# Sums of the attention weights behind the second half of P V, their rest on VectorE, in a four-layer cross-attention kernel

## The chip, the cores and the metric

The kernel runs on one core of a Trainium2 chip. The metric is the device time of one execution in microseconds (us). A core has five engines with instruction streams of their own: TensorE (PE; its weight loads are listed as PEld), VectorE (DVE), ScalarE (ACT), GpSimd (POOL) and SyncE (SP, which here issues the DMAs). They meet only at semaphores. PE writes to PSUM, in banks; DVE and ACT read those.

## What is computed

Four cross-attention layers run one after the other on x (4 batches, 512 tokens, 256 channels), each against the same context (4 batches, 1024 tokens, 512 channels). Layers 0, 2 and 3 are alike ("wide": 16 heads of 64), layer 1 has an RMS norm and grouped keys. Cut to what matters:

```python
def wide_layer(x, ctx, mask_A, mask_B, Wq, Wk, Wv, Wo, bo, tok_A, tok_B):
    q, k, v = x @ Wq, ctx @ Wk, ctx @ Wv                 # 16 heads of 64
    logits = einsum('bhqd,bhkd->bhqk', q, k) / 8
    logits += col_bias                                   # -20 * (1 - mask) in the columns tok_A, tok_B
    probs = softmax(logits, axis=-1)
    out = einsum('bhqk,bhkd->bhqd', probs, v)
    return out @ Wo + bo + x

x = wide_layer(x, ...)
x = x + attention(rmsnorm(x, norm_w) @ wq, ctx @ wk, ctx @ wv) @ wo   # 16 query heads, 4 key heads, of 16
x = wide_layer(x, ...)
x = wide_layer(x, ...)
```

The softmax is made as exp(logit - max), then P V, then a division by the sum of the exponentials over the 1024 keys. The change is about these sums.

## The kernel before

**Items and slots.** The work is cut into 112 items. A wide item p is a pair of heads for one batch (8 pairs x 4 batches in each wide layer); items 32 to 47 are the grouped layer. The program runs through slots s = -2 to 111. Slot s computes the scores, exponentials and first half of P V of item s, and finishes item s - 1 (second half of P V, sums, normalisation, output projection). It also projects queries and keys of item s + 2 and values of item s + 1, and takes the score maxima of item s + 1. Nothing is scheduled by a planner: each engine's stream is written out by hand, slot by slot.

**Turned slots.** All wide slots except 29 to 31 and 111 are of the form that the function turned_slot writes (111 is a shorter one of its own). On PE its order is: score block 0; the second half of P V of item s - 1 (attend, L1094, fp32, 16 matmuls); score block 1; the sums of item s - 1 (sums, L1140); then the projections of queries (project_q), keys (project_k) and values; score block 2; out projection and first half of P V; score block 3. A score block is four extra matmuls (L1039: minus the maximum and the token bias), two for the maxima of the next item ("opening", L986), twelve for the scores (L1054), and two more for maxima ("closing", L986).

**The sums.** POOL adds the eight blocks of exponentials into acc (add, L742). ACT then writes acc in f16 (sums_hi: acc_h, printed as tile sq, L1589). POOL subtracts this from acc and writes the rest in f16 (sums_lo: acc_l, also printed as sq, L754, semaphore s_acc_l). PE multiplies both by ones (L1140, 128*64 tiles) into a bank of ps_j. ACT copies that bank to rinv (sums_out, L1598, semaphore s_sum_sb), DVE takes the reciprocals (L2082), POOL multiplies o_un by them (L771). On ACT, sums_hi stands behind the exponentials of block 0, and sums_out behind the exponentials of block 1.

**P V.** The first half goes from PSUM to o_un by ACT; the second half is added to it by DVE (second_half, L2073, semaphore s_o_un), which frees its bank.

**Banks.** ps_j has two banks that nearly everything on PE takes in turn. bank_users lists the users in the order of PE's program with the bank of each (f, 1 - f, a, 1 - a: 0 or 1 by the slot's parity), and take puts a wait in front of each user for the reader of the bank's last user: s_o_un behind a second half of P V, s_sum_sb behind sums, s_max behind maxima, and so on. The opening maxima of a block use one bank of ps_j (kind "mx").

**Special slots.** For the first four items of a wide layer x is split in halves of precision in the same slots (splits_x); in slots 8 to 12 and 52 to 56 DVE also makes the token rows of a later layer, one step each (token_rows).

Of the kernel before, what the change touches and what calls it, by code (L numbers as in the profile page):

```python
# [15 lines left out]
ALU = mybir.AluOpType  # L16
# [41 lines left out]
def grouped(p):  # L58
    return G0 <= p < G1
# [107 lines left out]
def turned(s):  # L167

    return 0 <= s < N - 1 and not grouped(s) and not G0 - 3 <= s < G0


def splits_x(s):

    p = s + 2
    return p < N and not grouped(p) and p - STARTS[layer_of(p)] < B
# [22 lines left out]
def split_sums(p):  # L198

    return not grouped(p) and not G0 - 3 <= p < G0  # L200
# [9 lines left out]
    return sum(thirds(q) for q in range(p))  # L210


def splits(p):

    return wides(p) - min(max(p - (G0 - 3), 0), 3)
# [7 lines left out]
def bank_users():  # L223

    users = []
    turns = 0

    def then(kind, p, bank=None):
        users.append((kind, p, (1 - users[-1][2] if users else 0) if bank is None else bank))

    for s in range(-2, N):
        now, nxt, far, past = 0 <= s < N, 0 <= s + 1 < N, 0 <= s + 2 < N, 0 <= s - 1 < N
        if s == N - 1:
            then("pvb", s - 1, 0)
            then("sum", s - 1, 1)
            then("out0", s - 1, 0)
            then("out1", s - 1, 1)
            continue
        if turned(s):
            f = turns % 2  # L240
            turns += 1

            def opening(i, bank):
                for p, u in passes(s)[2 * i]:
                    then("mx", units(p) + u, bank)

            a = int(not splits_x(s)) ^ f
            opening(0, f)
            if far and splits_x(s):
                then("k0", s + 2, 1 - f)  # L250
            if past:
                then("sum" if grouped(s - 1) else "pvb", s - 1, a)
            opening(1, 1 - a)
            if past:
                then("rb" if grouped(s - 1) else "sum", s - 1, a)
            if far:
                then("q0", s + 2, 1 - a)
                if not splits_x(s):
                    then("k0", s + 2, 1 - f)
                then("k1", s + 2, f)  # L260
            if nxt:
                then("v0", s + 1, 1 - f)
            opening(2, f)
            if past:
                then("out0", s - 1, f)
            then("pva", s, 1 - f)
            opening(3, f)
            if nxt:
                then("v1", s + 1, 1 - f)
                then("nm0", s + 1, f)  # L270
            if past:
                then("out1", s - 1, f)
            continue
        if s == -1:
            for kind, p, bank in (("bias", 2, 0), ("v0", 0, 1), ("bias", 3, 0), ("bias", 4, 0), ("k0", 1, 1), ("bias", 5, 0),
                                  ("bias", 6, 0), ("k1", 1, 1), ("bias", 7, 0), ("q0", 1, 0), ("v1", 0, 1), ("nm0", 0, 0)):
                then(kind, p, bank)
            continue
        if not grouped(s):
            if rms_batch(s) is not None:  # L280
                then("ms", rms_batch(s), 0)
                then("pvb", s - 1, 1)
                then("k0", s + 2, 1)
            else:
                if past:
                    then("sum" if grouped(s - 1) else "pvb", s - 1)
                if far:
                    then("k0", s + 2)
            if s < 0:
                then("q0", s + 2)  # L290
                then("k1", s + 2)
            if past:
                then("rb" if grouped(s - 1) else "sum", s - 1)
            if s >= 0:
                if nxt and has_values(s + 1):
                    then("v0", s + 1)
                if far:
                    then("k1", s + 2)
                    if not late_queries(s):
                        then("q0", s + 2)  # L300
            if past:
                then("out0", s - 1)
            if now:
                then("pva", s)
            if past:
                then("out1", s - 1)
            if nxt and has_values(s + 1):
                then("v1", s + 1)
            if nxt and not grouped(s + 1):
                then("nm0", s + 1)  # L310
            if late_queries(s):
                then("q0", s + 2)
                then("q1", s + 2)
            if s == -2:
                then("bias", 0)
                then("bias", 1)
            continue
        if s == G0:
            then("pvb", s - 1, 0)
            then("k0", s + 2, 1)  # L320
            then("ms", rms_batch(s), 0)
            then("sum", s - 1, 0)
            then("v0", s + 1, 1)
            then("nm0", s, 0)
            then("nm1", s, 0)
            then("v1", s + 1, 0)
            then("k1", s + 2, 1)
            then("pv", s, 0)
            then("out0", s - 1, 1)
            then("out1", s - 1, 1)  # L330
            then("q0", s + 2, 1)
            then("q1", s + 2, 1)
            then("ms", rms_batch(s + 1), 1)
            continue
        if s > G0 + 1:
            then("out1", s - 2, 1)
        then("nm0", s, 1)
        then("nm1", s, 1)
        if has_values(s + 2):
            then("k0", s + 2, 1)  # L340
            then("sum", s - 1, 0)
            then("k1", s + 2, 1)
        else:
            then("sum", s - 1, 1)
        then("pv", s, 0)
        then("rb", s - 1, 1)
        if has_values(s + 1) and grouped(s + 1):
            then("v0", s + 1, 1)
        if early_bias(s) is not None:
            then("bias", early_bias(s), 1)  # L350
        then("q0", s + 2, 1)
        if has_values(s + 1) and grouped(s + 1):
            then("v1", s + 1, 1)
        if grouped(s + 2):
            then("q1", s + 2, 1)
        then("out0", s - 1, 1)
        if s == G1 - 1:
            then("out1", s - 1, 1)
            then("v0", s + 1, 1)
            then("v1", s + 1, 1)  # L360
            then("nm0", s + 1, 1)
    return users
# [8 lines left out]
def build(nc, a, out):  # L371
    with ExitStack() as ctx:
# [30 lines left out]
        acc = sb("acc", [P, 2, 2 * TQ], F32)  # L403
# [38 lines left out]
        acc_h, acc_l = halves[:, 0:2 * TQ], halves[:, 2 * TQ:4 * TQ]  # L442
# [246 lines left out]
        def _(pool):  # L689
# [108 lines left out]
            for s in range(-2, N - 1):  # L798
# [12 lines left out]
                splitting = s >= 0 and far and layer_of(s + 2) != GROUPED and s + 2 - STARTS[layer_of(s + 2)] < B  # L811
                if splitting:
                    split_x_hi(layer_of(s + 2), batch_of(s + 2))
                if past and split_sums(s - 1):
                    sums_lo(s - 1)
                if splitting:
                    split_x_lo(layer_of(s + 2), batch_of(s + 2))
# [33 lines left out]
        def _(pe):  # L851
# [299 lines left out]
            def rows_of_reciprocals(p):  # L1151

                pe.wait_ge(s_r_x, groups(p) + 1)
                dst = take("rb", p)
                for t in range(QT):
                    last = MM(dst[:, t * P:(t + 1) * P], rinv[:, t * P:(t + 1) * P], unit[:], start=True, stop=True)  # L1156
                last.then_inc(s_rb, 1)
# [114 lines left out]
            def turned_slot(s):  # L1272
# [20 lines left out]
                    project_k(s + 2, 0)  # L1293
                if past and not grouped(s - 1):
                    attend(s - 1, 1)
                elif past:
                    sums(s - 1)
                score_block(1)
                if past and not grouped(s - 1):
                    sums(s - 1)  # L1300
                elif past:
                    rows_of_reciprocals(s - 1)
                if far:
                    project_q(s + 2, 0)
                    if not splits_x(s):
# [616 lines left out]
        def _(dve):  # L1922
# [77 lines left out]
            def keys_lo(p, half):  # L2000
                r, keys = p % 3, slice(half * HALF, (half + 1) * HALF)
                dve.wait_ge(s_k_h, values_before(p) + 1 + half)
                if G1 <= p < G1 + 3:
                    dve.wait_ge(s_kb, 16 * builds_before(G1))
                to = all_keys(batch_of(p), half) if grouped(p) else k_l[:, r, keys]
                split_lo(to, bank(f"k{half}", p), 1 / WS, k_h[:, r, keys]).then_inc(s_k_l, 1)
# [56 lines left out]
            def extra_rows(p):  # L2063
# [2 lines left out]
                V.scalar_tensor_tensor(ext_q[:, p % 2, :], bank("nm0", p), flag(FLAG_M), bias_q[:], ALU.mult, ALU.add  # L2066
                                       ).then_inc(s_ext_q, 1)

            def second_half(p):
                dve.wait_ge(s_pvb, wides(p) + 1)  # L2070
                dve.wait_ge(s_pva_sb, wides(p) + 1)
                o = o_un[:, p % 2, :]
                V.tensor_tensor(o, bank("pvb", p), o, ALU.add).then_inc(s_o_un, 1)  # L2073
# [121 lines left out]
            def turned_slot(s):  # L2195
# [13 lines left out]
                        token_rows(w, s - start)  # L2209
                if far and splits_x(s):  # L2210
                    keys_lo(s + 2, 0)
                if past and not grouped(s - 1):
                    second_half(s - 1)
                elif past:
                    reciprocal_by_query(s - 1)
# [204 lines left out]
```

## Time and profile before

| What | us |
|---|---|
| median of 3 runs | 3433.31 |
| lowest, highest | 3433.3, 3434.82 |
| the profiled execution | 3431.57 |
| its span, first to last instruction | 3429.4 |
| PE busy in it | 3297.0 |
| DVE, POOL, ACT busy | 2537.5, 2497.7, 2194.5 |

The profile is of one execution. The page adds up busy times by engine and follows the chain of work that ended last; windows give the busy time of each engine in a stretch; timelines list instructions in order of time, neighbours of one form merged into one row, with the idle time before them in brackets and who ended it. PEclk is the granted clock of TensorE as a share of 2.4 GHz. A busy matmul's end is modelled; the distance from one start to the next is the safer measure.

### The profile page before, as it was taken

Reading aid. Unit: us, or ns where it says so; the run is one execution under the profiler, and the core shown is the slowest. Engines: PE = TensorE matmul, PEld = TensorE weight load, DVE = VectorE, ACT = ScalarE, POOL = GpSimd, SP = SyncE. Lnnn points to the kernel's source line nnn. Section 1 sums busy time; section 2 is a strip of 40 time slices with the busy share of each in tenths; the row PEclk is TensorE's granted clock in tenths of the full one; section 3 lists DMA queues with packets and bytes.
Section 4 is the critical chain, followed back from the end, with each engine's and each line's share of the span. In section 5 each row is a group of like instructions: output and inputs, shape, how many; then the busy total and the mean of one; then the engine's idle time right before and its main releaser. Section 6 shows DMA issues by size and latency. Waiting matters only on the chain.

```text
span 3429.4 us, 72971 instructions
## 1 busy us (share of the span) xinstructions
PE 3297.0 (96%) x28066; PEld 1558.9 (45%) x28066; DVE 2537.5 (74%) x4678; ACT 2194.5 (64%) x2698; POOL 2497.7 (73%) x1206
## 2 busy tenths in 40 slices
PE   6999999999987888889999999999999999999998
PEld 3444545445432322234454544445444544445553
DVE  6677877777766788856787777777667777777776
ACT  5466666666545677764666666666546666666665
POOL 6888888888741000028888888888888888888887
PEclk9999999999998999999999999999999999999999
DMA  4000000000000000000000000000000000000000
GB/s 157 1 11 11 1 11 11 11 2 9 6 10 12 8 13 17 17 1 11 11 1 11 11 11 2 11 11 11 1 11 11 1 11 11 11 2 11 3 2 26
DMA packets 50195, 42.29 MB, mean 12 GB/s; under 512 B 4928, under 2 KB 42176, under 8 KB 49856
## 3 DMA queue, kind: packets, MB, share of 16 engines
q1 hardware_dynamic: 49136, 37.08, 3.6%
q8 instruction: 231, 3.78, 0.5%
q14 instruction: 108, 0.88, 0.1%
q10 hardware_dynamic: 720, 0.53, 0.1%
HBM read 32.36 MB, written 2.10 MB: 10 GB/s over the span
## 4 chain that ended last, share of the span: by engine, by line
PE 90%; ACT 3%; DVE 3%; issue 2%; POOL 2%; DMA 0%; SPq 0%; ACTq 0%; DVEq 0%; POOLq 0%
PE ps_j L903 39%; PE ps_st L1054 13%; PE ps_j L1094 11%; PE ps_j L1107 6%; PE ps_sm L986 6%; PE ps_st L1039 3%; PE ps_j L1081 3%; ACT pt L1582 2%; PE ps_sm L1068 2%; PE ps_j L1140 1%; PE ps_st L986 1%; POOL acc L742 1%; PE ps_j L995 1%; PE ps_j L1156 1%; PE ps_j L1131 0%
## 5 line engine op out<-in xcount | busy, mean ns | idle before, releaser
L742 POOL TENSOR_TENSOR acc<-acc,pt 128x1024 f32<-128x1024 f32 x570 | 1365.0, 2395 | 261.9 <-ACT pt L1582 207.2
L1582 ACT ACTIVATE pt<-ps_st 128x1024 f32<-128x1024 f32 x768 | 742.9, 1019 | 300.8 <-PE ps_st L1054 288.9
L2045 DVE CUSTOM_DVE_ANT_0 ps_sm<-ps_sm,bias_m,nmx 128x512 f32<-128x512 f32 x666 | 479.9, 756 | 185.3 <-PE ps_j L986 149.3
L903 PE MATMUL ps_j<-w_h,ctx_h 128*128 128x128 f16 x3072 | 530.5, 219 | 2.3 <-ACT rinv L1598 1.1
L903 PE MATMUL ps_j<-w_l,ctx_h 128*128 128x128 f16 x3072 | 529.4, 219 | 0.0
L903 PE MATMUL ps_j<-w_h,ctx_l 128*128 128x128 f16 x3072 | 529.4, 219 | 0.0
L2045 DVE CUSTOM_DVE_ANT_0 ps_sm<-ps_sm,bias_m 128x512 f32<-128x512 f32 x486 | 334.7, 707 | 158.6 <-PE ps_j L986 147.3
L1094 PE MATMUL ps_j<-pt,v 128*64 128x512 f32 x1792 | 409.2, 598 | 1.3 <-DVE q_l L1933 1.3
L771 POOL TENSOR_TENSOR o_un<-o_un,rinv 128x512 f32<-128x512 f32 x111 | 142.0, 1280 | 336.9 <-ACT rinv L1594 291.1
L2082 DVE RECIPROCAL rinv<-rinv 128x256 f32<-128x256 f32 x190 | 331.3, 1746 | 14.1 <-ACT rinv L1598 4.4
L2035 DVE TENSOR_REDUCE nmg<-ps_st 128x2 f32<-128x1024 f32 x248 | 296.0, 1218 | 45.2 <-PE ps_st L986 43.8
L1582 ACT ACTIVATE pt<-ps_sm 128x1024 f32<-128x1024 f32 x256 | 261.4, 1021 | 101.5 <-PE ps_sm L1068 101.4
L903 PEld LDWEIGHTS ps_j<-w_h,ctx_h 128*128 128x128 f16 x3072 | 300.4, 98 | 55.6 <-issue 40.1
L903 PE MATMUL ps_j<-ctx_h,w_h 128*128 128x512 f16 x800 | 304.4, 380 | 16.9 <-DVE w_l L1933 12.7
L1559 ACT ACTIVATE p_h<-pt 128x1024 f16<-128x1024 f32 x312 | 319.7, 1052 | 0.0
L903 PEld LDWEIGHTS ps_j<-w_l,ctx_h 128*128 128x128 f16 x3072 | 300.7, 98 | 10.7
L903 PE MATMUL ps_j<-ctx_l,w_h 128*128 128x512 f16 x800 | 304.0, 380 | 0.0
L903 PE MATMUL ps_j<-ctx_h,w_l 128*128 128x512 f16 x800 | 303.8, 380 | 0.0
L986 PE MATMUL ps_sm<-k_h,q_h 64*128 64x512 f16 x1160 | 293.8, 380 | 9.2 <-DVE nmx L2045 6.9
L903 PEld LDWEIGHTS ps_j<-w_h,ctx_l 128*128 128x128 f16 x3072 | 300.6, 98 | 0.0
L754 POOL TENSOR_TENSOR sq<-acc,sq 128x1024 f16<-128x1024 f32 x92 | 198.6, 2159 | 118.4 <-ACT sq L1589 118.4
L1054 PE MATMUL ps_st<-q_h,k_l 64*128 64x512 f16 x1488 | 283.0, 377 | 0.0
(201 smaller groups left out, 6603.0 us busy)
## 6 DMA issues: line engine op xcount, KB each, us to landing
w_raw<-wk SPq DMA_DIRECT2D x25, 256.0 KB, 2.9
pt<-ctx_t SPq DMA_DIRECT2D x6, 1024.0 KB, 7.2
w_raw<-wv SPq DMA_DIRECT2D x24, 256.0 KB, 3.6
wo_raw<-wo SPq DMA_DIRECT2D x28, 128.0 KB, 2.0
w_raw<-wq SPq DMA_DIRECT2D x24, 128.0 KB, 3.0
k_h<-k_l SPq DMA_DIRECT2D x72, 32.0 KB, 2.0
x<-x_t SPq DMA_DIRECT2D x4, 512.0 KB, 8.3
acc<-ctx_t SPq DMA_DIRECT2D x2, 1024.0 KB, 9.1
```

The lines of the kernel that those rows point to most:

```text
L742: G.tensor_tensor(total, first, pt[:, n % RING, :], ALU.add).then_inc(s_acc, 1)
L754: G.tensor_tensor(acc_l, acc[:, p % 2, :], acc_h, ALU.subtract).then_inc(s_acc_l, 1)
L903: done = MM(dst, l, r, start=first and i == 0, stop=last and i == n - 1)
L986: last = MM(dst[h], queries_in(p, tile)[d, t * P:(t + 1) * P], k_h[d, r, half * HALF:(half + 1) * HALF], start=True, stop=True)
L1054: last = MM(ps_st[:, side, h, :], k[d, r, keys], q[d, r, :], start=False, stop=n == 2)
L1094: last = MM(dst[h * HD:(h + 1) * HD, :], values_of(p)[:, kt, h * HD:(h + 1) * HD], pt[:, (units(p) + kt) % RING, h * TQ:(h + 1) * TQ], sta ...
L1107: last = MM(dst[h * HD:(h + 1) * HD, :], v[:, p % 2, kt, h * HD:(h + 1) * HD], weights[:, h * TQ:(h + 1) * TQ], start=start, stop=stop)
L1559: A(p_h[:, kt, :], pt[:, n % RING, :], ACT.Copy).then_inc(s_p_h, 1)
L1582: A(pt[:, n % RING, :], src.rearrange("p h q -> p (h q)"), ACT.Exp).then_inc(s_exp, 1)
L2035: V.tensor_reduce(nmg[:, half, t, 2 * tile:2 * tile + 2], maxima_in(p, u), AX_X, ALU.max, negate=True).then_inc(s_max, 1)
L2045: last = V.tensor_tensor_reduce(out=src, in0=src, in1=bias_m[:, t, half * HALF:(half + 1) * HALF], scale=-1.0, scalar=nmx[:, 0, t, h:h + 1 ...
L2082: V.reciprocal(r, r).then_inc(s_rinv, 1)
```

## The change

In 84 slots (2 to 28, 50 to 77, 82 to 110; early_sums(s - 1) names them) three things are different:

- PE's sums of item s - 1 stand directly behind the second half of P V, ahead of score block 1. In bank_users the sums take bank 1 - a, and the opening maxima of block 1 take bank a, the other way round than before; q0 stays on 1 - a.
- acc_l is written by DVE, ahead of second_half, instead of by POOL.
- POOL waits for s_acc_l where its subtraction stood.

ACT's program is as it was.

```diff
--- before.py
+++ after.py
@@ -210,6 +210,11 @@
     return sum(thirds(q) for q in range(p))
 
 
+def early_sums(p):
+
+    return not grouped(p) and turned(p + 1) and not splits_x(p + 1)
+
+
 def splits(p):
 
     return wides(p) - min(max(p - (G0 - 3), 0), 3)
@@ -248,11 +253,16 @@
             opening(0, f)
             if far and splits_x(s):
                 then("k0", s + 2, 1 - f)
-            if past:
-                then("sum" if grouped(s - 1) else "pvb", s - 1, a)
-            opening(1, 1 - a)
-            if past:
-                then("rb" if grouped(s - 1) else "sum", s - 1, a)
+            if past and early_sums(s - 1):
+                then("pvb", s - 1, a)
+                then("sum", s - 1, 1 - a)
+                opening(1, a)
+            else:
+                if past:
+                    then("sum" if grouped(s - 1) else "pvb", s - 1, a)
+                opening(1, 1 - a)
+                if past:
+                    then("rb" if grouped(s - 1) else "sum", s - 1, a)
             if far:
                 then("q0", s + 2, 1 - a)
                 if not splits_x(s):
@@ -811,7 +821,9 @@
                 splitting = s >= 0 and far and layer_of(s + 2) != GROUPED and s + 2 - STARTS[layer_of(s + 2)] < B
                 if splitting:
                     split_x_hi(layer_of(s + 2), batch_of(s + 2))
-                if past and split_sums(s - 1):
+                if past and early_sums(s - 1):
+                    pool.wait_ge(s_acc_l, splits(s - 1) + 1)
+                elif past and split_sums(s - 1):
                     sums_lo(s - 1)
                 if splitting:
                     split_x_lo(layer_of(s + 2), batch_of(s + 2))
@@ -1293,13 +1305,13 @@
                     project_k(s + 2, 0)
                 if past and not grouped(s - 1):
                     attend(s - 1, 1)
-                elif past:
+                if past and (grouped(s - 1) or early_sums(s - 1)):
                     sums(s - 1)
                 score_block(1)
-                if past and not grouped(s - 1):
+                if past and grouped(s - 1):
+                    rows_of_reciprocals(s - 1)
+                elif past and not early_sums(s - 1):
                     sums(s - 1)
-                elif past:
-                    rows_of_reciprocals(s - 1)
                 if far:
                     project_q(s + 2, 0)
                     if not splits_x(s):
@@ -2066,6 +2078,10 @@
                 V.scalar_tensor_tensor(ext_q[:, p % 2, :], bank("nm0", p), flag(FLAG_M), bias_q[:], ALU.mult, ALU.add
                                        ).then_inc(s_ext_q, 1)
 
+            def sums_lo(p):
+                dve.wait_ge(s_acc_h, splits(p) + 1)
+                V.tensor_tensor(acc_l, acc[:, p % 2, :], acc_h, ALU.subtract).then_inc(s_acc_l, 1)
+
             def second_half(p):
                 dve.wait_ge(s_pvb, wides(p) + 1)
                 dve.wait_ge(s_pva_sb, wides(p) + 1)
@@ -2209,6 +2225,8 @@
                         token_rows(w, s - start)
                 if far and splits_x(s):
                     keys_lo(s + 2, 0)
+                if past and early_sums(s - 1):
+                    sums_lo(s - 1)
                 if past and not grouped(s - 1):
                     second_half(s - 1)
                 elif past:
```

PE in slot 26, from the second half of P V to the query projection (rows of the same form left out; s_sum_sb: rinv copied by ACT; s_o_un: second half added by DVE; s_acc_l: rest of acc written). Before:

```order
L1094 MATMUL ps_j<-pt,v 64x512 [waits s_x,s_v_sb,s_exp]
L1039 MATMUL ps_st<-ext_q,ext_k 128x512 [waits s_exp]
L986 MATMUL ps_sm<-k_h,q_h 128x512 [waits s_max,s_q_h,s_k_h]
L986 MATMUL ps_j<-k_h,q_h 128x512
L1054 MATMUL ps_st<-q_h,k_h 128x512 x2
L986 MATMUL ps_sm<-k_h,q_h 128x512 [waits s_max,s_q_h,s_k_h]
L986 MATMUL ps_sm<-k_h,q_h 128x512 [waits s_max_a]
L1140 MATMUL ps_j<-sq,ones_h_sb 64x512 [waits s_o_un,s_acc_l]
L1140 MATMUL ps_j<-sq,ones_h_sb 64x512 x3
L903 MATMUL ps_j<-xh,w_h 128x512 [waits s_max,s_xs,s_w_l]
L903 MATMUL ps_j<-xl,w_h 128x512
```

After, in the changed file's line numbers:

```order
L1106 MATMUL ps_j<-pt,v 64x512 [waits s_x,s_v_sb,s_exp]
L1152 MATMUL ps_j<-sq,ones_h_sb 64x512 [waits s_max,s_acc_l]
L1152 MATMUL ps_j<-sq,ones_h_sb 64x512 x3
L1051 MATMUL ps_st<-ext_q,ext_k 128x512 [waits s_exp]
L998 MATMUL ps_sm<-k_h,q_h 128x512 [waits s_max,s_o_un,s_q_h,s_k_h]
L998 MATMUL ps_j<-k_h,q_h 128x512
L1066 MATMUL ps_st<-q_h,k_h 128x512 x2
L998 MATMUL ps_sm<-k_h,q_h 128x512 [waits s_max,s_q_h,s_k_h]
L998 MATMUL ps_sm<-k_h,q_h 128x512 [waits s_max_a]
L915 MATMUL ps_j<-xh,w_h 128x512 [waits s_sum_sb,s_xs,s_w_l]
L915 MATMUL ps_j<-xl,w_h 128x512
```

The sums (ones_h_sb) moved up by one score block. The wait for s_o_un moved from the sums to the opening maxima, and the query projection (inputs xh,w_h) now waits for s_sum_sb, where it waited for s_max.

DVE in slot 26, from the closing maxima of block 0 to the first maxima of block 1. Before:

```order
L2045 ISA ps_sm,nmx<-ps_sm,bias_m,nmx 128x512 [waits s_max,s_bias_sb,s_nm16,s_max_mm]
L2045 ISA nmx 128x1
L2045 ISA ps_sm,nmx<-ps_sm,bias_m,nmx 128x512
L2045 ISA nmx 128x1
L2073 TENSOR_TENSOR o_un<-ps_j,o_un 128x512 [waits s_pva_sb,s_pvb]
L2045 ISA ps_sm,nmx<-ps_sm,bias_m 128x512 [waits s_bias_sb,s_max_mm]
```

After:

```order
L2057 ISA ps_sm,nmx<-ps_sm,bias_m,nmx 128x512 [waits s_max,s_bias_sb,s_nm16,s_max_mm]
L2057 ISA nmx 128x1
L2057 ISA ps_sm,nmx<-ps_sm,bias_m,nmx 128x512
L2057 ISA nmx 128x1
L2083 TENSOR_TENSOR sq<-acc,sq 128x1024 [waits s_acc_h]
L2089 TENSOR_TENSOR o_un<-ps_j,o_un 128x512 [waits s_pva_sb,s_pvb]
L2057 ISA ps_sm,nmx<-ps_sm,bias_m 128x512 [waits s_bias_sb,s_max_mm]
```

One subtraction (sq is acc_l, written from acc and acc_h) came in between the maxima and second_half (o_un).

POOL in slot 26, from the last adds of item 25 to the normalisation (o_un). Before:

```order
L742 TENSOR_TENSOR acc<-acc,pt 128x1024 [waits s_acc,s_exp] x4
L754 TENSOR_TENSOR sq<-acc,sq 128x1024 [waits s_acc_h]
L742 TENSOR_TENSOR acc<-pt 128x1024 [waits s_sum,s_exp]
L742 TENSOR_TENSOR acc<-acc,pt 128x1024 [waits s_acc,s_exp] x2
L771 TENSOR_TENSOR o_un<-o_un,rinv 128x512 [waits s_o_un,s_rinv]
```

After:

```order
L752 TENSOR_TENSOR acc<-acc,pt 128x1024 [waits s_acc,s_exp] x4
L752 TENSOR_TENSOR acc<-pt 128x1024 [waits s_sum,s_exp,s_acc_l]
L752 TENSOR_TENSOR acc<-acc,pt 128x1024 [waits s_acc,s_exp] x2
L781 TENSOR_TENSOR o_un<-o_un,rinv 128x512 [waits s_o_un,s_rinv]
L759 TENSOR_TENSOR p_l<-pt,p_h 128x1024 [waits s_p_h]
```

The subtraction is gone, and the first add of item 26 waits for s_acc_l too.

## Rows read from the trace of the kernel before

**Rows 1.** Page: busy us by engine, and the chain that ended last

```profile
PE 3297.0 (96%) x28066; PEld 1558.9 (45%) x28066; DVE 2537.5 (74%) x4678; ACT 2194.5 (64%) x2698; POOL 2497.7 (73%) x1206
...
PE 90%; ACT 3%; DVE 3%; issue 2%; POOL 2%; DMA 0%; SPq 0%; ACTq 0%; DVEq 0%; POOLq 0%
```

**Rows 2.** Windows: length, busy (count) of PE, PEld, DVE, ACT, POOL; then PEclk

```profile
794.85:824.15 29.30, 29.21 (x262) 14.61 (x261) 21.99 (x45) 19.41 (x25) 25.05 (x13) 1.00 0.01 2
```

**Rows 3.** Timeline of PE, slot 26: start, us, engine, line, [idle before]

```profile
818.41 3.65 PE L1094 MATMUL ps_j<-pt,v 128*64 128x512 f32 x16
...
821.99 0.40 PE L1039 MATMUL ps_st<-ext_q,ext_k 32*128 32x512 f16 x4
...
822.32 0.39 PE L986 MATMUL ps_sm<-k_h,q_h 64*128 64x512 f16 x1
...
823.84 0.38 PE L986 MATMUL ps_sm<-k_h,q_h 64*128 64x512 f16 x2
...
824.15 0.62 PE L1140 MATMUL ps_j<-sq,ones_h_sb 128*64 128x512 f16 x4
...
824.71 0.39 PE L903 MATMUL ps_j<-xh,w_h 128*128 128x512 f16 x1
...
833.97 0.40 PE L1039 MATMUL ps_st<-ext_q,ext_k 32*128 32x512 f16 x4
```

**Rows 4.** Timeline of DVE, slot 26

```profile
819.87 0.14 DVE L2045 DVE_READ_ACCUMULATOR2_ANT nmx<- 128x1 f32 x1
...
822.11 0.69 DVE L2073 TENSOR_TENSOR o_un<-ps_j,o_un 128x512 f32<-128x512 f32 x1 [2.10 <-PE ps_j L1094]
...
830.27 2.35 DVE L2026 TENSOR_TENSOR pt<-ps_st,p_h 128x1024 f16<-128x1024 f32 x2
```

**Rows 5.** Timeline of ACT, slot 26

```profile
819.48 1.06 ACT L1589 ACTIVATE sq<-acc 128x1024 f16<-128x1024 f32 x1
...
823.40 1.94 ACT L1582 ACTIVATE pt<-ps_st 128x1024 f32<-128x1024 f32 x2 [0.97 <-PE ps_st L1054]
...
825.22 0.61 ACT L1598 ACTIVATE rinv<-ps_j 128x512 f32<-128x512 f32 x1
```

**Rows 6.** Timeline of POOL, slot 26

```profile
820.61 2.13 POOL L754 TENSOR_TENSOR sq<-acc,sq 128x1024 f16<-128x1024 f32 x1 [1.37 <-ACT sq L1589]
```

**Rows 7.** Timeline of PE, slot 26, a change of tile shape

```profile
839.42 0.38 PE L1107 MATMUL ps_j<-pt,v_h 128*64 128x512 f16 x2
839.73 0.39 PE L1039 MATMUL ps_st<-ext_q,ext_k 32*128 32x512 f16 x4
```

**Rows 8.** Durations in ns of two DVE lines, min/median/max

```profile
L1946 DVE TENSOR_TENSOR xl<-x,xh x1: 1226/1226/1226, 17.6 to 17.6; 128x1024 f16<-128x1024 f32 x1
L2073 DVE TENSOR_TENSOR o_un<-ps_j,o_un x95: 691/692/692, 87.2 to 3402.8; 128x512 f32<-128x512 f32 x95
```

**Rows 9.** Timeline of DVE, slot 10: a token row

```profile
351.07 1.28 DVE L1990 SCALAR_TENSOR_TENSOR y_rms<-iota_sb,tok_f,y_rms 128x1024 f16<-128x1024 f16 x1
```

**Rows 10.** Timeline, slot 32: DVE's second_half, and PE waiting for it

```profile
944.75 0.69 DVE L2073 TENSOR_TENSOR o_un<-ps_j,o_un 128x512 f32<-128x512 f32 x1 [4.02 <-PE ps_j L1094]
945.59 0.38 PE L903 MATMUL ps_j<-ctx_h,w_h 128*128 128x512 f16 x1 [0.89 <-DVE o_un L2073]
```

**Rows 11.** Timeline of PE's weight loads, slot 26

```profile
825.94 0.10 PEld L903 LDWEIGHTS ps_j<-ctx_h,w_h 128*128 128x128 f16 x1 [0.26 <-issue]
```

**Rows 12.** Timeline of ACT and PE, slot 110

```profile
3378.18 0.61 ACT L1598 ACTIVATE rinv<-ps_j 128x512 f32<-128x512 f32 x1
3378.84 0.23 PE L903 MATMUL ps_j<-w_h,ctx_h 128*128 128x128 f16 x1 [1.11 <-ACT rinv L1598]
```

**Rows 13.** Windows of two stretches with waits, in the grouped layer

```profile
1036.00:1063.00 27.00, 18.93 (x94) 4.54 (x91) 18.88 (x20) 12.23 (x15) 4.66 (x5) 0.77 0.05 11
1096.00:1104.00 8.00, 5.83 (x61) 3.23 (x58) 4.37 (x5) 5.71 (x7) 3.40 (x2) 1.00 0.07 17
```

## The prediction

> **What bounds the kernel now.** I read the page's busy times and its chain first [rows 1]: PE is busy for 96% of the span, and 90% of the chain that ended last is PE. Then one slot of the steady state in the windows [rows 2]: 29.21 of 29.30 us are PE's, at granted clock 1.00. So in these slots anything that makes PE wait is added to the time in full, and only what shortens PE's own row is a gain; DVE, ACT and POOL have 7 us, 10 us and 4 us spare. Then the timelines of slot 26, engine by engine, around the place that is edited [rows 3, 4, 5]. The reader should see in [rows 3] that PE never idles there: attend, score block 1, sums and the query projection follow each other. The sums start at 824.15 us, long after their data: POOL's acc_l ends at 820.61 + 2.13 = 822.74 [rows 6].
>
> 84 slots are edited (2 to 28, 50 to 77, 82 to 110). Nearly all look like slot 26; slots that differ are treated below.
>
> **PE's own work.** Nothing is added or taken away; the four sums move. A pair of 512-column f16 matmuls costs 0.215 us within one tile shape, and 0.31 us where the shape changes, as from L1107 to L1039 (839.42 to 839.73) [rows 7]. Before, the changes are attend to extra scores, maxima to sums, sums to queries: three. After: sums to extra scores and maxima to queries, since attend and sums both have 128*64: two. So some 0.09 us per slot would be saved, if nothing waited. The Trainium skill (TensorEngine Tiling (Array Packing), Key Properties) says that changing the tiling mode drains the engine; by it alone the sum would be 84 x 0.09 = 8 us less, and the trace agrees on the price of a change. The rows above would give the same, and it is the fast rival below.
>
> **acc_l on DVE instead of POOL.** ACT's acc_h ends at 819.48 + 1.06 = 820.54 [rows 5]. DVE has nothing between 820.01 (819.87 + 0.14) and 822.11 [rows 4]. Its nearest operation of this form, L1946 (128x1024, f16 from f32, two SBUF inputs), took 1.226 us [rows 8]. From the 820.61 at which POOL started, it ends at 821.84. The first sums can then go at about 821.99, when attend's last step is over [rows 3]; at best 0.1 us earlier. second_half on DVE starts at 822.11 as before: margin 0.27 us. Price of the move: nothing in the common slot. It is hidden by attend (3.58 us, 818.41 to 821.99), and without that cover it would cost its 1.23 us. In the slots with a token row in front, L1990 runs on DVE from 351.07 for 1.28 us [rows 9], 0.9 us past the usual end of DVE's work there. Then acc_l ends some 0.2 us after second_half should start. That is six slots (steps 2 to 4, two layers), 1 to 2 us in all.
>
> POOL loses 2.13 us of work per slot and gets a wait for s_acc_l ahead of add 1. Behind it stand adds 2 and 3, the normalisation, output_lo and adds 4 to 7. The wait ends at 821.84, before POOL got to add 1 in the kernel before (822.74), so nobody sees it; POOL is not the bound.
>
> One more check: DVE's second_half now runs beside POOL's add instead of POOL's acc_l. It took 691 to 692 ns in all 95 cases [rows 8], and in slot 26 it lay inside POOL's two-input subtraction until 822.74 [rows 6]. So I add nothing. The Trainium skill (SBUF — State Buffer, Who interferes with whom) has a DVE instruction with two SBUF inputs contend with GpSimd's reads, and one with a single SBUF input not. By that rule the moved subtraction is the one at risk; with POOL held there is nobody to collide with, so it too adds nothing.
>
> **The two banks that change hands.** This is where the sum is decided. ps_j has two banks, and whoever takes one waits for the reader of its last user. In the listed order the sums and the maxima of block 1 swap banks. Two waits move with them.
>
> First, the opening maxima of block 1 now take the bank of P V, so they wait for s_o_un, DVE's second_half. That ends at 822.11 + 0.69 = 822.80 [rows 4]. Where PE was seen waiting for just this (L903 after L2073), it started 0.15 us after the end: 944.75 + 0.69 = 945.44 against 945.59 [rows 10]. So the maxima start at 822.95. PE itself would be there at 821.99 + 0.56 (the sums, as from 824.15 to 824.71) + 0.33 (the extra scores) = 822.88, or 822.78 if attend's last step shrinks. The wait is 0.07 to 0.17 us. In the kernel before the maxima started at 822.32, so score block 1 is now 0.63 us late, of which the sums themselves are 0.56.
>
> Second, and far larger: the query projection took the bank of the maxima (s_max, long done); now it takes the bank of the sums, and waits for s_sum_sb, ACT's copy of the sums into rinv. ACT's program is not edited. The copy stands behind both exponentials of block 1: they start at 823.40 and run into the copy at 825.22, which takes 0.61 [rows 5]. That the sums are ready 2 us sooner does not help. Worse, the exponentials follow PE's scores of block 1, which are 0.63 later. So:
> - exponentials of block 1 at 823.40 + 0.63 = 824.03;
> - copy to rinv at 825.22 + 0.63 = 825.85, end 826.46;
> - from the end of this copy to the first matmul: as large as 0.14 us or as small as 0.05. In slot 26 the weight load of the key projection, which waited for the same semaphore with two others, came at 825.94 [rows 11], 0.11 after 825.83, and its matmul some 0.03 later; in slot 110 the first matmul came at 3378.84 after 3378.18 + 0.61 = 3378.79, where the wait stood alone [rows 12]. In the new order it is again one of three waits, so 0.14: start at 826.60;
> - before, the projection started at 824.71 [rows 3]. Lateness per slot: 1.89 us.
>
> PE has nothing else in its queue to do meanwhile: from the end of the maxima (822.95 + 1.52 + 0.31 = 824.78) to 826.60 it stands for 1.8 us. Slot 110 of the kernel before shows this very wait, since no projection lay between there: PE idle 1.11 us, put down to ACT rinv L1598 [rows 12].
>
> **What is behind it.** Nothing after the projection catches up, for PE has 0.09 us of slack per slot [rows 2]. Nothing else becomes a new wait either: the reciprocals follow the copy (0.63 us late), q_l and k_l follow PE's projections (1.89 late), so no step on DVE, ACT or POOL is more than 1.89 us late when the block of PE that needs it is 1.89 us late as well. The nearest such meeting is DVE's weights' rests, which end at 830.27 + 2.35 = 832.62 for the extra scores at 833.97 [rows 3, 4]; those 1.35 us stay.
>
> **Sum.** Slot 110 has no query projection behind its sums; it only gets block 1's delay, 0.6 us. The other 83 slots: 83 x 1.89 = 156.9. Token slots: 1.3. Together 158.8 us. The profiled execution took 3431.57 us (span 3429.4), so it would take 3590.4; the median of the runs is 1.74 us above the profiled one, so **3592.1 us**, 4.6% slower. Bounds: without the wait for s_o_un and with the short latency it is 1.89 - 0.17 - 0.09 = 1.63 us per slot, 3570.5; with DVE's subtraction lengthened by 0.4 us in each slot (second_half 0.13 later and a little more), 3606.
>
> **Rivals.**
> - The fast one: the copy to rinv is not in the way, PE only saves a change of tile shape. For it speaks [rows 7]; it gives 3433.3 - 84 x 0.09 = 3426. It decides if s_sum_sb is there by 824.79. But the copy would have to stand ahead of the exponentials on ACT, and it doesn't. 3%.
> - Only the wait for s_o_un counts: 84 x (0.63 - 0.56 + 0.01) = 7 us, 3440, about the edge of what can be told. It needs the same condition. 3%.
> - The stall also costs clock. In the stretch 1036 to 1063, with PE busy 18.93 of 27 us, the granted clock was 0.77; in 1096 to 1104, which has a wait of 1.83 us, it was 1.00 [rows 13]. The Trainium skill (TensorE: Matmul & The Clock Gate, Why this matters for your kernels) warns of idle gaps between bursts. If each stall of 1.8 us put the following 3 us to 1.2 GHz (level 0.50), each slot would lose 1.5 us more: 3592 + 126 = 3718. Against it: a wait of the same length left the clock at 1.00. 3%.
> - The change does what it says and I have missed a cover, so that half the wait remains: 3513. 2%.
>
> **Chances.** Forecast 89%. The range 3570 to 3608 is the forecast's own, with its bounds; it leaves out the rivals, 11%. A measurement tells 0.2% (7 us) from no change: faster 3%, same 3%, slower 94%.
>
> **What would show it.** The slot period goes from 29.30 to 31.19 us. In PE's groups (line numbers of the changed file), L915 with inputs xh,w_h has an idle time of about 83 x 1.8 = 149 us, released by ACT rinv; the maxima at L998 some 0.1 us each, released by DVE o_un. The new subtraction on DVE takes 1.2 us and 84 of it stand there; second_half doesn't wait for it. PE clock stays 1.00. I'm wrong if PE's projection starts within 0.5 us of the last maxima, if the clock falls, or if DVE's subtraction takes over 1.5 us.

## The result, and the profile after

| What | before | after |
|---|---|---|
| median, us | 3433.31 (4 runs) | 3591.97 (4 runs) |
| lowest, highest | 3432.93, 3434.82 | 3591.7, 3593.49 |
| the profiled execution | 3431.57 | 3592.16 |
| its span | 3429.4 | 3590.1 |
| mean granted clock | 0.995 | 0.995 |

After stands to before as 1.0462 (95% interval 1.0445 to 1.0478): 4.6% slower. The forecast was 3592.1 us, range 3570 to 3608.

The page of the kernel after: busy times with their share of the span, then the shares of the chain that ended last.

```profile
PE 3299.6 (92%) x28066; PEld 1572.9 (44%) x28066; DVE 2673.0 (74%) x4762; ACT 2194.4 (61%) x2698; POOL 2326.2 (65%) x1122
PE 83%; ACT 7%; issue 5%; DVE 3%; POOL 2%; DMA 0%; ACTq 0%; SPq 0%; DVEq 0%; POOLq 0%
```

Against [rows 1], PE is as busy in us (3299.6, before 3297.0), but its share fell from 96% to 92%. In the chain PE lost 7 points, and ACT and "issue" took them: ACT's instructions and the way from them to PE now lie on the path.

The window that ends at the sums of slot 26, from the sums of one slot to those of the next (columns: stretch, its length, busy us of PE, PEld, DVE, ACT and POOL with the number of instructions, PEclk, DMA share, GB/s).

```profile
837.00:868.18 31.18, 29.22 (x264) 14.78 (x264) 23.66 (x45) 19.41 (x25) 23.06 (x12) 1.00 0.01 2
```

The slot is 31.18 us long instead of 29.30 [rows 2], with the same 29.2 us of work on PE and the clock at 1.00. What is new is idle time.

The timelines of slot 26, PE, ACT, DVE and POOL in turn. The slot's second half of P V starts at 864.68, before at 818.41 [rows 3]; so 46.27 us taken off any of these times give its place in the slot of before.

```profile
864.68 3.65 PE L1106 MATMUL ps_j<-pt,v 128*64 128x512 f32 x16
868.17 0.60 PE L1152 MATMUL ps_j<-sq,ones_h_sb 128*64 128x512 f16 x4
868.70 0.39 PE L1051 MATMUL ps_st<-ext_q,ext_k 32*128 32x512 f16 x4
869.22 0.37 PE L998 MATMUL ps_sm<-k_h,q_h 64*128 64x512 f16 x1
870.73 0.40 PE L998 MATMUL ps_sm<-k_h,q_h 64*128 64x512 f16 x2
872.87 0.38 PE L915 MATMUL ps_j<-xh,w_h 128*128 128x512 f16 x1 [1.75 <-ACT rinv L1610]
...
865.75 1.06 ACT L1601 ACTIVATE sq<-acc 128x1024 f16<-128x1024 f32 x1
870.30 1.94 ACT L1594 ACTIVATE pt<-ps_st 128x1024 f32<-128x1024 f32 x2 [1.60 <-PE ps_st L1066]
872.12 0.60 ACT L1610 ACTIVATE rinv<-ps_j 128x512 f32<-128x512 f32 x1
...
866.85 1.23 DVE L2083 TENSOR_TENSOR sq<-acc,sq 128x1024 f16<-128x1024 f32 x1 [0.56 <-ACT sq L1601]
868.38 0.69 DVE L2089 TENSOR_TENSOR o_un<-ps_j,o_un 128x512 f32<-128x512 f32 x1 [0.31 <-PE ps_j L1106]
...
868.15 2.35 POOL L752 TENSOR_TENSOR acc<-pt 128x1024 f32<-128x1024 f32 x1 [2.61 <-DVE sq L2083]
```

Read it as a chain. The sums (L1152) start at 868.17 and have all they need. The last maxima of block 1 (L998) start at 870.73. Then PE stands until 872.87, when the query projection (L915) goes. What it waits for ended 0.15 us before: ACT's copy to rinv (L1610), 872.12 + 0.60 = 872.72. That copy had its data some 3 us earlier; it stood behind the two exponentials of block 1 (870.30, 1.94 long for both). The sums came early and their reader did not.

In the whole trace: the waits (engine, what waited, for what: us in total, times, longest), and PE's group of the first query projection.

```profile
PE ps_j L915 <- ACT rinv L1610: 145.0, 83, 1.8
POOL acc L752 <- DVE sq L2083: 223.6, 84, 3.2
L915 PE MATMUL ps_j<-xh,w_h 128*128 128x512 f16 x256 | 97.8, 382 | 154.9 <-ACT rinv L1610 145.0 <-ACT acc L1565 2.6 <-ACT bias_m L1674 1.7
```

83 waits of 1.75 us make 145 of the 160.7 us that the span gained (3590.1 less 3429.4). POOL waits longer in sum (223.6 us, for DVE's subtraction), and this costs nothing. A large idle time on an engine that isn't the bound is no finding.

### The profile page after: what moved, and what is told of

The parts are those of the page before. It is cut to its first block, busy times and chain, and to the rows that moved or that the text cites. A ratio compares the mean times of both kernels' runs of the same rounds, so it can differ in the third digit from the quotient of the medians.

```text
span 3590.1 us, 72973 instructions
## 1 busy us (share of the span) xinstructions
PE 3299.6 (92%) x28066; PEld 1572.9 (44%) x28066; DVE 2673.0 (74%) x4762; ACT 2194.4 (61%) x2698; POOL 2326.2 (65%) x1122
## 4 chain that ended last, share of the span: by engine, by line
PE 83%; ACT 7%; issue 5%; DVE 3%; POOL 2%; DMA 0%; ACTq 0%; SPq 0%; DVEq 0%; POOLq 0%
PE ps_j L915 38%; PE ps_st L1066 11%; PE ps_j L1106 10%; PE ps_j L1119 6%; PE ps_sm L998 5%; ACT pt L1594 4%; PE ps_st L1051 3%; PE ps_j L1093 3%; PE ps_sm L1080 2%; PE ps_st L998 1%; POOL acc L752 1%; ACT rinv L1610 1%; PE ps_j L1152 1%; PE ps_j L1007 1%; PE ps_j L1168 0%
## 5 line engine op out<-in xcount | busy, mean ns | idle before, releaser
L915 PE MATMUL ps_j<-w_h,ctx_h 128*128 128x128 f16 x3072 | 530.5, 219 | 1.2 <-DVE k_l L1945 0.7
L915 PE MATMUL ps_j<-w_l,ctx_h 128*128 128x128 f16 x3072 | 529.4, 219 | 0.0
L915 PE MATMUL ps_j<-w_h,ctx_l 128*128 128x128 f16 x3072 | 529.4, 219 | 0.0
L752 POOL TENSOR_TENSOR acc<-pt 128x1024 f32<-128x1024 f32 x95 | 223.4, 2351 | 238.1 <-DVE sq L2083 223.6
L915 PEld LDWEIGHTS ps_j<-w_h,ctx_h 128*128 128x128 f16 x3072 | 300.4, 98 | 54.6 <-issue 40.2
L915 PE MATMUL ps_j<-ctx_h,w_h 128*128 128x512 f16 x800 | 304.3, 380 | 17.1 <-DVE w_l L1945 13.0
L998 PE MATMUL ps_sm<-k_h,q_h 64*128 64x512 f16 x1160 | 294.1, 379 | 19.2 <-DVE nmx L2057 6.9
L915 PEld LDWEIGHTS ps_j<-w_l,ctx_h 128*128 128x128 f16 x3072 | 300.7, 98 | 10.7
L915 PE MATMUL ps_j<-ctx_l,w_h 128*128 128x512 f16 x800 | 304.0, 380 | 0.0
L915 PE MATMUL ps_j<-ctx_h,w_l 128*128 128x512 f16 x800 | 303.9, 380 | 0.0
L915 PEld LDWEIGHTS ps_j<-w_h,ctx_l 128*128 128x128 f16 x3072 | 300.6, 98 | 0.0
```

Source lines behind the costliest of these rows:

```text
L752: G.tensor_tensor(total, first, pt[:, n % RING, :], ALU.add).then_inc(s_acc, 1)
L915: done = MM(dst, l, r, start=first and i == 0, stop=last and i == n - 1)
L998: last = MM(dst[h], queries_in(p, tile)[d, t * P:(t + 1) * P], k_h[d, r, half * HALF:(half + 1) * HALF], start=True, stop=True)
```

## The experiments

The first three are the kernel after with one thing changed. The fourth and the sixth are the first one (ACT's copy ahead) with one thing more. The fifth is the kernel before with one part of the change. Ratios are to the kernel before, run beside them: 3432.62 us (19 runs) with the first four, 3432.91 us (12 runs) with the last two. Slot periods are read between the starts of the second half of P V in neighbouring slots.

**One: the copy ahead of the exponentials.** Theory: ACT's order costs 1.75 us per slot. Rival: the sums' new place is itself slow (tile shapes, banks, memory of DVE and POOL), and PE would wait for something else.

```diff
+                if past and early_sums(s - 1):
+                    sums_out(s - 1)
                 exponentials_of(1)
-                if past:
+                if past and not early_sums(s - 1):
                     sums_out(s - 1)
```

> The changed kernel, but in the 84 slots ACT copies the sums to rinv ahead of the two exponentials of block 1 instead of behind them. If the query projection's wait for this copy is the cause (1.83 of the 1.88 us per slot), PE's projection starts straight behind the maxima, and what is left is the wait of the opening maxima for DVE's second half, 0.07 us per slot, plus 2 us in the slots with token rows: about 3441 us. If the cause is something else in the new order (bank order, DVE's longer program, POOL held), it stays near 3592 us.

Measured: 3441.84 us (9 runs), ratio 1.0028 (1.0018 to 1.0038). One window and the timelines of PE and ACT:

```profile
795.42:824.79 29.37, 29.16 (x262) 14.70 (x262) 23.11 (x45) 19.52 (x25) 22.99 (x12) 1.00 0.01 2
...
824.79 0.60 PE L1152 MATMUL ps_j<-sq,ones_h_sb 128*64 128x512 f16 x4
825.33 0.39 PE L1051 MATMUL ps_st<-ext_q,ext_k 32*128 32x512 f16 x4
825.85 0.37 PE L998 MATMUL ps_sm<-k_h,q_h 64*128 64x512 f16 x1
827.68 0.39 PE L915 MATMUL ps_j<-xh,w_h 128*128 128x512 f16 x1
...
825.43 0.60 ACT L1610 ACTIVATE rinv<-ps_j 128x512 f32<-128x512 f32 x1
826.92 1.94 ACT L1594 ACTIVATE pt<-ps_st 128x1024 f32<-128x1024 f32 x2 [0.89 <-PE ps_st L1066]
```

The copy now fills a gap of ACT before the exponentials, and the projection follows the maxima directly. 150 of the 159 us are gone by the place of one instruction on ACT. The slot is 29.37 us, still 0.07 above [rows 2]. What is left is in PE's rows: from the extra scores (825.33) to the opening maxima (825.85) it takes 0.52 us, where before it was 0.33 (821.99 to 822.32 [rows 3]). These 0.19 are the wait for DVE's second_half; the saved change of tile shape gives some 0.10 back. No run gives the projection the other bank and leaves ACT's order alone, so this shows that moving the copy is enough, and not that it is the only cure.

**Two: the copy between the exponentials.** If the delay is the copy's place and nothing else, one exponential in front of it must cost about half.

```diff
-                exponentials_of(1)
-                if past:
+                if past and early_sums(s - 1):
+                    exponentials(s, 2)
                     sums_out(s - 1)
+                    exponentials(s, 3)
+                else:
+                    exponentials_of(1)
+                    if past:
+                        sums_out(s - 1)
```

> The changed kernel, but ACT copies the sums between the two exponentials of block 1. If PE's lateness follows the place of the copy, the projection starts 0.97 us later than in the kernel before instead of 1.88: 83 x 0.97 + 3433 + 4 = 3518 us, half way. If the place of the copy doesn't matter, 3592 us.

Measured: 3515.1 us (2 runs), ratio 1.0238 (1.022 to 1.0257). ACT, PE, and the wait over the whole trace:

```profile
879.76 1.02 ACT L1594 ACTIVATE pt<-ps_st 128x1024 f32<-128x1024 f32 x1 [1.59 <-PE ps_st L1066]
880.68 0.59 ACT L1610 ACTIVATE rinv<-ps_j 128x512 f32<-128x512 f32 x1
881.41 0.38 PE L915 MATMUL ps_j<-xh,w_h 128*128 128x512 f16 x1 [0.83 <-ACT rinv L1610]
...
PE ps_j L915 <- ACT rinv L1610: 68.9, 83, 0.8
```

The wait went from 1.75 to 0.83 us, by the 0.92 us from one exponential to what follows it. With none, one and two exponentials ahead the slots are 29.37, 30.26 and 31.18 us. Each exponential ahead of the copy adds its 0.9 us to the slot.

**Three: POOL not held.** The change has POOL wait for DVE's subtraction. Is that hold needed, or does it only look careful?

```diff
-                if past and early_sums(s - 1):
-                    pool.wait_ge(s_acc_l, splits(s - 1) + 1)
-                elif past and split_sums(s - 1):
+                if past and split_sums(s - 1) and not early_sums(s - 1):
                     sums_lo(s - 1)
```

> The changed kernel without POOL's wait for s_acc_l (POOL's next add doesn't touch what DVE subtracts). If DVE's subtraction with two SBUF inputs and POOL's add exclude each other for whole instructions, POOL's add starts 0.9 us ahead of DVE's subtraction and lasts 2.35 us, the subtraction ends some 1.4 us late or is stretched to 2.7 us, second_half and the opening maxima follow 1.1 us late: 84 x 1.1 = 94 us, 3686 us. If they don't disturb each other, 3592 us and the subtraction stays at 1.23 us.

Measured: 3708.1 us (2 runs), ratio 1.0801 (1.0781 to 1.082), 116 us above the kernel after. POOL, DVE and PE in one of the common slots, the subtraction over the whole trace (ns, min/median/max), and the wait:

```profile
839.85 2.37 POOL L752 TENSOR_TENSOR acc<-pt 128x1024 f32<-128x1024 f32 x1 [0.43 <-ACT pt L1592]
840.75 2.56 DVE L2081 TENSOR_TENSOR sq<-acc,sq 128x1024 f16<-128x1024 f32 x1 [0.56 <-ACT sq L1599]
843.36 0.62 PE L1150 MATMUL ps_j<-sq,ones_h_sb 128*64 128x512 f16 x4 [1.12 <-DVE sq L2081]
...
L2081 DVE TENSOR_TENSOR sq<-acc,sq x84: 1209/2559/2564, 118.1 to 3649.5; 128x1024 f16<-128x1024 f32 x84
PE ps_j L1150 <- DVE sq L2081: 109.5, 84, 2.4
```

POOL's add runs from 839.85 to 842.22. DVE's subtraction is there at 840.75 and its record ends at 843.31: from the end of the add that is 1.09 us, about what the whole subtraction takes alone (1.23). So DVE did next to nothing in the 1.47 us in which both were there. POOL's add took 2.37 us, alone 2.35: it lost nothing. The Trainium skill (SBUF — State Buffer, Who interferes with whom) calls the shared ports an exclusive lock between DVE and GpSimd; the trace agrees, and shows that the one that came second paid in full. In the kernel after, the hold keeps the same subtraction at 1215 to 1226 ns in all 84 cases:

```profile
L2083 DVE TENSOR_TENSOR sq<-acc,sq x84: 1215/1225/1226, 115.9 to 3532.7; 128x1024 f16<-128x1024 f32 x84
```

I had expected 94 us over the kernel after and got 116. The common slots are 32.30 us long, 1.12 above the kernel after, as expected (1.1): 94 us over 84 slots. The rest sits in two places. Twenty slots, mostly every fourth, are 0.33 us longer than that (32.63 for a common one): 7 us. And eight of the slots with token rows (9 to 12, 53 to 56) are 33.9 to 35.0 us long, together 16 us more than those of the kernel after with 1.12 added to each. There PE's wait for the subtraction reaches the 2.4 us shown as the longest. Slot 110 gives 1 us back.

**Four: copy first, and block 1's maxima one pair of scores later.** This takes away the wait that the first experiment left, by giving PE 0.22 us of other work in front of it.

```diff
-            def turned_scores(p, i):
+            def turned_scores(p, i, between=None):
...
+                        if between and side == 0 and n == 0:
+                            between()
...
+                    if i == 1 and past and early_sums(s - 1):
+                        turned_scores(s, i, open_block)
+                    else:
+                        open_block()
+                        turned_scores(s, i)
```

(open_block issues the opening maxima; the copy stands first on ACT, as in the first experiment.)

> As the run with the copy first, and PE issues the first pair of block 1's score matmuls ahead of the opening maxima, so that the maxima come 0.22 us later and no longer wait for DVE's second half. If that wait eats what the saved change of tile shape gives (the sums start 0.43 us after the last step of P V, where the next matmul before started 0.52 us after it), the projection comes 0.085 us earlier than in the kernel before, 84 times: 3433 - 7 + 2 (token slots) = 3428 us. If the saving was not real, or the closing maxima wait instead, 3434 to 3445 us.

Measured: 3427.41 us (11 runs), ratio 0.9983 (0.9974 to 0.9992). It is the one version that beats both kernels, if by 5 us (0.17%, with the interval clear of 1).

```profile
793.78:822.96 29.18, 29.09 (x263) 14.70 (x263) 23.00 (x45) 19.52 (x25) 23.01 (x12) 1.00 0.01 2
...
822.96 0.60 PE L1154 MATMUL ps_j<-sq,ones_h_sb 128*64 128x512 f16 x4
823.49 0.39 PE L1051 MATMUL ps_st<-ext_q,ext_k 32*128 32x512 f16 x4
823.82 0.39 PE L1066 MATMUL ps_st<-q_h,k_h 64*128 64x512 f16 x2
824.04 0.38 PE L998 MATMUL ps_sm<-k_h,q_h 64*128 64x512 f16 x1
```

Steps of 0.33 and 0.22 us, and no wait. The slot is 29.18 us, 0.12 less than [rows 2]: the saved change of tile shape is real. 0.10 of it is the step from attend to the sums, 0.02 the sums themselves (822.96 to 823.49, 0.53 us, against 0.56 in [rows 3]). The 77 common slots give 9.1 us. The six slots with a token row in front give 2.3 back: they are 29.6 to 29.8 us long, since DVE's subtraction comes late there. Slots 81 and 110 give back 0.3 and 0.2. The last 1 us or so lies in stretches that no edit touches; in the profiled execution the start and the grouped layer alone took 3.2 us more than before's.

**Five: DVE's subtraction and POOL's hold alone.** PE's order and the banks are those of the kernel before. (early_sums and DVE's sums_lo are added as in the change.)

```diff
-                if past and split_sums(s - 1):
+                if past and early_sums(s - 1):
+                    pool.wait_ge(s_acc_l, splits(s - 1) + 1)
+                elif past and split_sums(s - 1):
                     sums_lo(s - 1)
...
+                if past and early_sums(s - 1):
+                    sums_lo(s - 1)
                 if past and not grouped(s - 1):
                     second_half(s - 1)
```

> The kernel before, with only the subtraction moved to DVE and POOL held for it; the sums, the banks and ACT's copy as before. If the move itself costs nothing (it fits DVE's gap, and POOL is not the bound), 3433 to 3435 us, the 1 to 2 us being the slots with token rows. If DVE's longer program or POOL's hold were part of the loss, several tens of us more.

Measured: 3433.49 us (10 runs), ratio 1.0 (0.999 to 1.0009). In DVE's groups:

```profile
L2078 DVE TENSOR_TENSOR sq<-acc,sq 128x1024 f16<-128x1024 f32 x84 | 102.9, 1225 | 36.7 <-ACT sq L1596 36.7
```

84 subtractions, 102.9 us more on DVE and 171 us less on POOL (busy 2327.0 us, before 2497.7), and the time is that of before: every common slot is 29.30 us, and so are the six with a token row, where 1 to 2 us had been expected in all. The cover is real, and so the loss is in the order and the banks. Two slots of this trace do differ: slot 81 is 0.3 us longer and slot 110 is 1.2; both come up again below.

**Six: copy first, subtraction on POOL.** Does the early place of the sums need DVE at all? (ACT's part of the diff is that of the first experiment.)

```diff
-                if past and early_sums(s - 1):
-                    pool.wait_ge(s_acc_l, splits(s - 1) + 1)
-                elif past and split_sums(s - 1):
+                if past and split_sums(s - 1):
                     sums_lo(s - 1)
...
-                if past and early_sums(s - 1):
-                    sums_lo(s - 1)
                 if past and not grouped(s - 1):
                     second_half(s - 1)
```

> The run with the copy first, but the subtraction back on POOL, where it ends 0.9 us after the end of the second half of P V. If the early sums need DVE's subtraction, PE waits for s_acc_l: sums 0.95 us later, and with them the maxima and the query projection: 84 x 0.87 = 73 us over the kernel before, 3506 us. If the wait is absorbed in the one for s_o_un behind it, about 3441 us.

Measured: 3504.85 us (4 runs), ratio 1.0212 (1.0194 to 1.023). PE, POOL, and the wait:

```profile
838.98 3.65 PE L1104 MATMUL ps_j<-pt,v 128*64 128x512 f32 x16
843.38 0.62 PE L1150 MATMUL ps_j<-sq,ones_h_sb 128*64 128x512 f16 x4 [0.74 <-POOL sq L764]
...
841.19 2.13 POOL L764 TENSOR_TENSOR sq<-acc,sq 128x1024 f16<-128x1024 f32 x1 [1.37 <-ACT sq L1599]
PE ps_j L1150 <- POOL sq L764: 64.8, 84, 1.1
```

POOL needs 2.13 us where DVE needs 1.23, and attend hides only DVE's. So moving the subtraction earns nothing by itself (experiment five), but with the subtraction on POOL the early sums cost 63 us more than with it on DVE (experiment one).

| Kernel | slot, us | median, us | ratio |
|---|---|---|---|
| before | 29.30 | 3432.62 | 1 |
| after | 31.18 | 3591.97 | 1.0462 |
| one: copy first | 29.37 | 3441.84 | 1.0028 |
| two: copy between | 30.26 | 3515.1 | 1.0238 |
| three: POOL not held | 32.30 | 3708.1 | 1.0801 |
| four: copy first, maxima later | 29.18 | 3427.41 | 0.9983 |
| five: subtraction alone | 29.30 | 3433.49 | 1.0 |
| six: copy first, POOL subtracts | 30.11 | 3504.85 | 1.0212 |

The median in the row of before is the one that ran with experiments one to four; each ratio is to before's median of its own group (3433.31 for after, 3432.91 for five and six).

## Why the prediction was right, point by point

**The bound and its place.** PE has no slack in the steady slots, so a wait there is paid in full. Shown: 1.88 us more per slot, and 29.2 us of PE's work as before.

**The copy behind the exponentials.** This was the term that decided, and it held to 0.01 us. The maxima were put at 822.95, which is 869.22 in the trace of after, and that is where they start. The projection was put at 826.60, that is 872.87: it starts at 872.87, with 0.15 us from the end of the copy (0.14 taken). Experiments one and two show that the copy's place is the cause, and not only near it. Of the signs that were named, the projection's idle time was put at 149 us and is 145.0. The one for the maxima (0.1 us each, put down to DVE o_un) is in no list of waits; the wait shows only in the distance of the starts.

**Its parts.** Some of them were off, and cancelled. The sums were to start with attend's last step at about 821.99; they start at 821.90 in that scale (868.17), as the prediction allowed for. The step from attend's last matmul to the next one is 0.42 us where both have tile shape 128*64, and 0.525 us where the shape changes, and the sums take 0.53 us and not 0.56. So PE reached the opening maxima earlier, and the wait for second_half was 0.19 us, above the 0.07 to 0.17 given: from 868.70 the maxima would go at 869.03 and went at 869.22. Their start hangs on DVE alone, so it stayed where it was put.

**Nothing catches up.** Nearly: a slot is 1.877 us longer where 1.89 was told. The projections behind the late start take 9.247 us instead of 9.262.

**DVE's subtraction.** 1.23 us as taken from [rows 8], not slowed, hidden in the common slots. Experiment five has it alone at no cost there.

**The token slots.** 0.2 us each was too little. The token row [rows 9] is followed by the subtraction, and PE's sums wait for that. DVE and PE in such a slot:

```profile
397.82 1.28 DVE L2004 SCALAR_TENSOR_TENSOR v_rms<-iota_sb,tok_f,v_rms 128x1024 f16<-128x1024 f16 x1
399.02 1.22 DVE L2083 TENSOR_TENSOR sq<-acc,sq 128x1024 f16<-128x1024 f32 x1
400.29 0.62 PE L1152 MATMUL ps_j<-sq,ones_h_sb 128*64 128x512 f16 x4 [0.28 <-DVE sq L2083]
```

The sums are 0.45 us late, and the six slots cost 1.9 us beyond the common ones (told: 1.3). The failed step was to time the subtraction against second_half, which it delays a little. I should have timed it against the sums, which were now to start 0.2 us earlier than second_half. Experiment five bears this out: there the subtraction delays only second_half, and the token slots are 29.30 us like the others.

**Slot 110** cost 1.5 us where 0.6 was told. Block 2 starts 0.62 us later after attend than before (13.79 against 13.17 us), as told. The other 0.87 us lie between the starts of blocks 2 and 3, where PE does the same work at a lower granted clock. The first rows of block 2 and the windows up to block 3, for before, after and experiment five:

```profile
3384.53 0.40 PE L1039 MATMUL ps_st<-ext_q,ext_k 32*128 32x512 f16 x4 [2.84 <-DVE pt L2026]
3384.53:3391.80 7.27, 7.27 (x47) 2.65 (x48) 3.44 (x9) 2.88 (x4) 7.27 (x4) 0.77 0.01 2
...
3544.31 0.62 PE L1051 MATMUL ps_st<-ext_q,ext_k 32*128 32x512 f16 x4 [4.51 <-DVE pt L2038]
3544.31:3552.45 8.14, 8.14 (x48) 2.74 (x49) 3.44 (x9) 2.19 (x3) 8.00 (x5) 0.67 0.01 2
...
3385.49 0.61 PE L1046 MATMUL ps_st<-ext_q,ext_k 32*128 32x512 f16 x4 [2.84 <-DVE pt L2033]
3385.49:3393.95 8.46, 8.46 (x47) 2.80 (x48) 3.49 (x9) 2.19 (x3) 8.32 (x5) 0.64 0.01 2
```

The mean granted clock is 0.77 before, 0.67 after and 0.64 in experiment five, and the stretch takes 7.27, 8.14 and 8.46 us. In part of it pairs of 512-column matmuls start 0.43 us apart instead of 0.215 (3385.38 and 3385.81 in before), which is the level of 1.2 GHz. Experiment five has the same order on PE and the same idle time in front (2.84 us) as before, and still loses 1.19 us. So the runs don't show that the 0.87 is owed to the change.

**The sum.** On the profiled executions the term was 158.8 us and 160.6 were measured (160.7 in the span): 83 slots 155.8, token slots 1.9 beyond that, slot 110 1.5, and 1.5 elsewhere, of which 0.9 in the grouped layer, 0.3 at the start and 0.3 in slot 81. The grouped layer's stretch differs by about 1 us either way from one kernel's execution to another's (1.2 us shorter in experiment five, where nothing of it is changed), so this can't be put down to the edit. Slot 81 is 0.3 us longer in all six kernels where DVE subtracts and in neither of the two where POOL does; the slot's own code is not edited, and why is open. That the median came within 0.2 us of the forecast has luck in it: 1.8 us were missing from the sum, and the 1.74 added for before's median over its profiled execution have no counterpart after, whose median lies 0.19 us below.

**The rivals.** The fast one needed the copy ahead of the exponentials. With that order given to it (experiment one), it is still 9 us slower than before and not 7 faster, since the wait for second_half stays (0.07 us in a common slot) and the token slots cost 2.3 us; only experiment four, which removes both waits, is faster. The second rival, the wait for second_half alone, is experiment one: 7 us were forecast and 9.2 measured. The missed cover that halves the wait did not come: the wait is 1.75 us a slot. Nor did the clock rival. The Trainium skill (TensorE: Matmul & The Clock Gate, Why this matters for your kernels) warns of idle gaps between bursts; in the window above the granted clock is 1.00, the upper level of 2.4 GHz, in spite of the stall, and 83 such stalls left the mean at 0.995. The lower level is seen in slot 110, behind an idle time of 2.84 us in before and 4.51 us in after.

## What to carry to other kernels

When work changes its place in a rotation of buffers, list for each next user of each buffer whom it waits for now, and then look where that reader stands in its own engine's order; a result that is ready early is worth nothing if its reader is not moved too. An experiment that moves only the reader tells at once whether the order or the work is at fault. And time an operation that is moved against the earliest thing that now needs it, not against its new neighbour.

## What the runs showed of the hardware that I had not expected

A DVE subtraction of two SBUF inputs that started 0.90 us into a POOL addition made next to no headway until the addition had ended: 2.56 us instead of 1.23, with the addition at 2.37 instead of 2.35. The expectation had left open whether it would be recorded as late or as stretched; it is stretched, and POOL's addition is not. The recorded duration of the DVE instruction holds this wait, so in a profile it reads as a slow instruction and not as an idle engine. second_half, with one SBUF input, beside POOL's add took 0.69 us as ever.

A change of tile shape costs PE about 0.10 us, between f16 matmuls (0.31 against 0.215 us [rows 7]) and after fp32 ones (0.525 against 0.42 us). It looks like nothing, and at 84 slots it is the whole gain of the best version.
